# First expert layer: rows stored by token and gathered by index, in place of rows scattered to their expert

## The reference

```
gates = softmax(xf @ Wg.T)                 # xf: 2048 tokens x 256, layer-normed
topw, topi = top_k(gates, 2)
C = 538                                    # capacity of an expert
e_ord = topi.T.reshape(-1)                 # all first choices, then all second choices
cnt = position of each entry among those of its expert, in that order
buf[e, pos] = xf[token]        where cnt < C
y = gelu(buf @ W1 + b1) @ W2 + b2          # per expert: 538 rows, 256 -> 1024 -> 256
out[token] = sum over its 2 choices of topw * y[e, pos] * (cnt < C)
```

## Time and profile before

| what | us |
|---|---|
| median of 3 runs (lowest, highest) | 1897.67 (1895.84, 1907.63) |
| profiled execution, device time | 1896.24 |
| its span, first to last instruction | 1894.4 |
| PE busy in it | 1618.7 |
| DVE busy in it | 1081.3 |
| ACT busy in it | 905.7 |
| POOL busy in it | 795.1 |

### The profile page before, as it was taken

The page is one execution under the profiler, slowest core; times in us unless marked ns, Lnnn a source line. Parts: engine busy times, 40 slices in busy tenths (PEclk is TensorE's granted clock), DMA queues, the critical chain, the costliest instruction groups (busy, mean ns, idle before and its releaser), DMA issues.

```text
span 1894.4 us, 26189 instructions
## 1 busy us (share of the span) xinstructions
PE 1618.7 (85%) x9225; PEld 1114.1 (59%) x9225; DVE 1081.3 (57%) x2202; ACT 905.7 (48%) x1474; POOL 795.1 (42%) x740
## 2 busy tenths in 40 slices
PE   5954999968976999856996987999999999997997
PEld 3444999946744333346993665555555655563774
DVE  5762556567966355532545797565656666644335
ACT  2422445413346998723443664555454455431463
POOL 3053211223542554421005564576665666744106
PEclk9776999979998999968998987999999999998999
DMA  9613233030000000062113000000000000022454
GB/s 363 232 67 100 80 136 134 24 119 1 1 22 1 1 7 7 14 286 78 46 46 106 1 1 34 1 0 1 1 0 1 1 1 1 0 79 74 127 162 133
DMA packets 61879, 117.76 MB, mean 62 GB/s; under 512 B 7247, under 2 KB 50499, under 8 KB 59064
## 3 DMA queue, kind: packets, MB, share of 16 engines
q1 hardware_dynamic: 53688, 95.90, 14.5%
q0 software_dynamic: 8064, 20.19, 3.3%
HBM read 72.26 MB, written 44.89 MB: 62 GB/s over the span
## 4 chain that ended last, share of the span: by engine, by line
PE 65%; DVE 16%; POOL 6%; issue 5%; ACT 4%; DMA 4%; SPq 0%; POOLq 0%; DVEq 0%; ACTq 0%
PE psum L166 60%; DMA arena<-xb 2%; DVE arena L2399 2%; POOL arena L870 2%; DVE rounded L2328 2%; DVE arena L171 1%; DVE arena L1734 1%; POOL xb L1057 1%; POOL arena L1852 1%; PE psum L206 1%; DVE arena L2475 1%; DVE arena L187 1%; PE psum L682 1%; DVE arena L1964 1%; ACT arena L1616 1%
## 5 line engine op out<-in xcount | busy, mean ns | idle before, releaser
L166 PE MATMUL psum<-arena 128*128 (+14 forms) x5084 | 1015.3, 433 | 115.6 <-DVE arena L1725 20.5
L166 PEld LDWEIGHTS psum<-arena 128*128 128x128 f32 (+3 forms) x5084 | 586.1, 174 | 439.3 <-issue 288.1
L166 PE MATMUL psum<-rounded 128*128 128x256 f32 (+7 forms) x3072 | 531.0, 338 | 6.0 <-ACT rounded L1573 1.4
L166 PEld LDWEIGHTS psum<-rounded 128*128 128x128 f32 (+3 forms) x3072 | 407.4, 186 | 137.5 <-issue 53.3
L2503 POOL TENSOR_TENSOR arena<-arena 128x1024 f32<-128x1024 f32 (+1 forms) x111 | 262.9, 2369 | 128.7 <-ACT arena L2453 124.3
L2399 DVE TENSOR_REDUCE arena<-psum 128x1 f32<-128x512 f32 x256 | 163.5, 681 | 95.6 <-PE psum L166 94.2
L2453 ACT ACTIVATE arena<-psum 128x1024 f32<-128x1024 f32 x144 | 147.3, 1024 | 141.8 <-PE psum L166 141.1
L1616 ACT ACTIVATE arena<-psum,arena 128x1024 f32<-128x1024 f32 x128 | 134.5, 1116 | 21.8 <-PE psum L166 20.5
L870 POOL DMA_INDIRECT arena<-yb,arena x48 | 46.0, 958 | 211.9 <-DMA yb<-arena 198.4
L1210 POOL DMA_INDIRECT yt<-arena x40 | 39.8, 996 | 183.5 <-DVE arena L1173 178.0
L918 DVE SCALAR_TENSOR_TENSOR rounded<-arena,rounded 128x540 fp32r<-128x540 f32 (+1 forms) x96 | 81.8, 885 | 33.5 <-ACT rounded L1119 32.4
(11 more groups left out here) (269 smaller groups left out, 1894.0 us busy)
## 6 DMA issues: line engine op xcount, KB each, us to landing
arena<-in_w SPq DMA_DIRECT2D x8, 2048.0 KB, 8.7
arena<-xb SPq DMA_DIRECT2D x70, 128.0 KB, 2.2
yb<-arena SPq DMA_DIRECT2D x70, 128.0 KB, 1.7
arena<-in_w1u SPq DMA_DIRECT2D x4, 2048.0 KB, 15.4
xb<-arena SPq DMA_DIRECT2D x3, 2048.0 KB, 16.0
xb<-arena SPq DMA_DIRECT2D x2, 2064.0 KB, 31.7
arena<-xb SPq DMA_DIRECT2D x8, 516.0 KB
yt<-arena SPq DMA_DIRECT2D x2, 2048.0 KB, 15.2
```

The costliest lines, as they stand in the source:

```text
L166: return e.matmul(o, l, r, start=start, stop=stop, skip_group_check=True)
```

## The change

- `xb0` is now 4096 rows of 256 in the order of pairs (row 256t + 2p + k, the same row for both choices k) and 128 rows of zeros behind. SP writes it with two DMAs for each tile as soon as the tile is normed (32 DMAs of 128 KB). Only the 128 rows of zeros are blanked ahead.
- In place of slot numbers, DVE makes for each pair its block (expert times 5 + rank div 128, of 40) and its place in the block (`dve_columns0`), and a matrix of marks, 128 tokens x 128 places (`dve_marks0`). PE multiplies marks with columns that hold 16 - t and 2p + k in the block's column (`pe_marks0`, 32 products of 128 x 80, all summed in one bank), and DVE reads off the table of pair numbers by slot, 128 x 40 (`dve_ids0`). Slots without a pair get 4096, the first row of zeros.
- POOL gathers each expert's rows by that table, five indirect DMAs of 128 rows (`pool_rows0`), those of experts 0 to 2 ahead of the first result scatter, those of x + 2 ahead of expert x's result scatters. SP's `load_rows` is gone, and so are the 32 scatters.
- The same table serves the scatters of results.

The diff, without the changes of counts in later layers and the views that only name memory:

```diff
...
@@ -109,7 +109,7 @@
-        xb0, yt0 = dram("xb0", RXA, RW), dram("yt0", 2 * 128 * NT)
+        xb0, yt0 = dram("xb0", 2 * 128 * NT + 128), dram("yt0", 2 * 128 * NT)
         xb1, yb1 = dram("xb1", NB1 * 128), dram("yb1", NB1 * 128)
...
@@ -235,11 +235,11 @@
         z_tile = oR + 7680
-        N_ZERO = 16 * (3 + 2 + 3 + 2)
+        N_ZERO = 16 * (1 + 2 + 3 + 2)
...
             e.wait_ge(s_zsrc, 1)
-            for buf, rows, n in ((xb0, RXA, RW), (yt0, 2 * 128 * NT, 256), (xb1, NB1 * 128, 256), (xb3, NB3 * 128, 256)):
+            for buf, rows, n in ((xb0[2 * 128 * NT:], 128, 256), (yt0, 2 * 128 * NT, 256), (xb1, NB1 * 128, 256), (xb3, NB3 * 128, 256)):
                 bv = buf.rearrange("(a p) n -> p a n", p=128)
@@ -266,8 +266,8 @@
             settle(e, dve, e.tensor_reduce(NBD, cst("tri"), AX.X, ALU.add))
-            settle(e, dve, e.tensor_scalar(NBD, NBD, 2.0, GONE + 2.0, ALU.mult, ALU.add))
-            e.tensor_scalar(IDS, bc(cst("iota")[:, 0:NT], 2, 2), 256.0, NBD, ALU.mult, ALU.subtract)
+            for k in range(2):
+                e.tensor_scalar(PLACE[:, k:k + 1], NBD, -2.0, k - 2.0, ALU.mult, ALU.add)
             e.wait_ge(s_gate, 1)
@@ -657,10 +657,6 @@
                 pool_rstd(e, 16 + t + 1, t)
-            e.wait_ge(s_slot, 1)
-            e.wait_ge(s_zero, N_ZERO)
-            pool_scatter0(e, 0, 8)
...
@@ -894,8 +889,14 @@
         BACK_TILES = {0: 1, 1: 1, 2: 2, 4: 2, 6: 2, 8: 4, 12: 4}
-        BACK0 = dict(zip(BACK_TILES, [(s, 16) for s in s_rout] + [(s, 144) for s in s_rin[:2]] + [(s, 16) for s in s_rin[2:]]))
-        s_xg = sem("rows_blank")
+        BACK0 = dict(zip(BACK_TILES, [(s, 16) for s in s_rout] + [(s, 272) for s in s_rin[:2]] + [(s, 16) for s in s_rin[2:]]))
+        s_ip = sem("ids_product")
+        f0_m = o + 8192
+        f0_MK, f0_CL = (view(f0_m + a, n).bitcast(BF16).rearrange("p (c r) -> p c r", c=32) for a, n in ((0, 2048), (2048, 1280)))
+        f0_HIT, f0_RAMP = view(f0_m + 3328, 320).bitcast(BF16).rearrange("p (c r) -> p c r", c=16), view(f0_m + 3648, 64).bitcast(BF16)
+        f0_J40, f0_A4, f0_LIM = view(f0_m + 3712, 40), view(f0_m + 3760, 16, 4), view(f0_m + 3752, 4)
+        f0_A, f0_R = view(f0_m + 3824, 32), view(f0_m + 3856, 16).bitcast(BF16)
+        f0_AT = view(f0_m + 3880, 40)
         s_w1a, s_w1d, s_w2a, s_w2d = sem("w1_hi"), sem("w1_lo"), sem("w2_hi"), sem("w2_lo")
@@ -951,7 +952,7 @@
             xg = f0_Xg[:, x % 2]
-            e.wait_ge(s_rin[x % 2], 32 * (x // 2 + 1))
+            e.wait_ge(s_sct[x % 2], 80 * (x // 2 + 1))
             for k in range(2):
@@ -1042,38 +1043,60 @@
             settle(e, dve, e.tensor_reduce(f0_POS[:, cs], f0_T[i].rearrange("p e t -> p t e"), AX.X, ALU.add))
-            e.tensor_scalar(f0_BIG[:, cs], f0_POS[:, cs], float(CAP), 1e6, ALU.is_ge, ALU.mult)
-            settle(e, dve, e.scalar_tensor_tensor(out=f0_TO[:, cs], in0=f0_MI[:, cs], scalar=-float(CAP), in1=f0_POS[:, cs],
-                                                  op0=ALU.mult, op1=ALU.add))
-            settle(e, dve, e.scalar_tensor_tensor(out=f0_TO[:, cs], in0=f0_BIG[:, cs], scalar=8.0 * CAP, in1=f0_TO[:, cs],
-                                                  op0=ALU.add, op1=ALU.add))
-            e.tensor_copy(f0_IS[:, cs], f0_TO[:, cs]).then_inc(s_slot, 1)
-        def pool_scatter0(e, a, b):
-            for c in range(a, b):
-                e.indirect_dma_start(
-                    xb0, bass.IndirectOffsetOnAxis(f0_IS[:, c:c + 1], 0), XN[:, c % NT, :], None,
-                    bounds_check=8 * CAP - 1, oob_is_err=False).then_inc(s_sct[c // NT], 16)
-        def pool_second_ids0(e, half):
-            v = IDS[:, 8 * half:8 * half + 8, :]
-            e.wait_ge(s_sct[0], 16 * 8 * (half + 1))
-            settle(e, pool, e.tensor_scalar(v, v, 1.0, None, ALU.add))
-        def pool_ids0(e, x):
-            e.wait_ge(s_rin[x % 2], 32 * (x // 2 + 1))
-            if x == 0:
-                e.wait_ge(s_xg, 1)
-            settle(e, pool, e.tensor_scalar(f0_ID[:, x, :], f0_Xg[:, x % 2, :, 256], float(GONE), None, ALU.add))
-            e.sem_inc(s_ids, 1)
+        def dve_ramps0(e):
+            io = cst("iota")
+            for a, n in ((0, 48), (48, 48), (96, 32)):
+                e.tensor_scalar(f0_RAMP[:, a:a + n], io[:, 0:n], float(a), None, ALU.add)
+            e.tensor_scalar(f0_J40, io[:, 0:40], -40.0, None, ALU.add)
+            settle(e, dve, e.tensor_scalar(f0_LIM, io[:, 1:5], 128.0, None, ALU.mult))
+        def dve_columns0(e, i):
+            cs, k = PART_COLS[i], i // 2
+            n = cs.stop - cs.start
+            pos, blk, j, hit, cl = f0_POS[:, cs], f0_A[:, cs], f0_TO[:, cs], f0_HIT[:, 0:n, :], f0_CL[:, cs, :]
+            e.tensor_scalar(f0_BIG[:, cs], pos, float(CAP), 1e6, ALU.is_ge, ALU.mult)
+            settle(e, dve, e.tensor_tensor(f0_A4[:, 0:n, :], bc(pos, 2, 4), bc(f0_LIM, 1, n), ALU.is_ge))
+            settle(e, dve, e.tensor_reduce(blk, f0_A4[:, 0:n, :], AX.X, ALU.add))
+            e.scalar_tensor_tensor(out=f0_R[:, cs], in0=blk, scalar=-128.0, in1=pos, op0=ALU.mult, op1=ALU.add)
+            settle(e, dve, e.scalar_tensor_tensor(out=j, in0=f0_MI[:, cs], scalar=-5.0, in1=blk, op0=ALU.mult, op1=ALU.add))
+            settle(e, dve, e.tensor_tensor(j, j, f0_BIG[:, cs], ALU.add))
+            settle(e, dve, e.tensor_tensor(hit, bc(f0_J40, 1, n), bc(j, 2, 40), ALU.is_equal))
+            e.tensor_tensor(cl[:, :, 0:40], bc(cst("desc")[:, PART_TILES[i]], 2, 40), hit, ALU.mult)
+            settle(e, dve, e.tensor_scalar(cl[:, :, 40:80], hit, PLACE[:, k:k + 1], None, ALU.mult))
+        def dve_marks0(e, i):
+            cs = PART_COLS[i]
+            e.tensor_tensor(f0_MK[:, cs, :], bc(f0_RAMP, 1, cs.stop - cs.start), bc(f0_R[:, cs], 2, 128),
+                            ALU.is_equal).then_inc(s_slot, 1)
+        def pe_marks0(e, i):
+            e.wait_ge(s_slot, i + 1)
+            for c in range(PART_COLS[i].start, PART_COLS[i].stop):
+                m = mm(e, psum[:, 5, 0:80], f0_MK[:, c, :], f0_CL[:, c, :], c == 0, c == 31)
+            if i == 2:
+                m.then_inc(s_ip, 1)
+        def dve_ids0(e):
+            e.wait_ge(s_ip, 1)
+            settle(e, dve, e.tensor_scalar(f0_AT, psum[:, 5, 0:40], -256.0, 256.0 * NT, ALU.mult, ALU.add))
+            e.tensor_tensor(f0_ID.rearrange("p x a -> p (x a)"), psum[:, 5, 40:80], f0_AT, ALU.add).then_inc(s_ids, 1)
+        def pool_rows0(e, x):
+            if x >= 2:
+                e.wait_ge(s_tu, 3 * (x - 1))
+            for a in range(5):
+                e.indirect_dma_start(f0_Xg[:, x % 2, a, :], None, xb0,
+                                     bass.IndirectOffsetOnAxis(f0_ID[:, x, a:a + 1], 0)).then_inc(s_sct[x % 2], 16)
...
             pe_ranks0(e, 2)
+            for i in range(3):
+                pe_marks0(e, i)
             pe_rows(e, 0)
@@ -1124,13 +1147,21 @@
         def dve_ffn0(e):
+            dve_ramps0(e)
+            dve_columns0(e, 0)
             dve_best0(e, 1)
             e.sem_inc(s_gx, 1)
+            dve_marks0(e, 0)
             dve_place0(e, 1)
             dve_best0(e, 2)
-            dve_place0(e, 2)
             GT = f0_IDF[:, 1, :].rearrange("p (k t) -> p k t", k=2)
             e.tensor_tensor(GT, f0_M, bc(f0_M[:, 0, :], 1, 2), ALU.subtract).then_inc(s_gx, 1)
+            dve_columns0(e, 1)
+            dve_marks0(e, 1)
+            dve_place0(e, 2)
+            dve_columns0(e, 2)
+            dve_marks0(e, 2)
+            dve_ids0(e)
             e.tensor_scalar(f0_WI, f0_POS, float(CAP), None, ALU.is_lt)
@@ -1139,7 +1170,6 @@
                                                   in1=f0_WI.rearrange("p (k t) -> p k t", k=2), op0=ALU.mult, op1=ALU.mult))
-            e.memset(f0_Xg[:, :, 4, :], 0.0).then_inc(s_xg, 1)
             e.wait_ge(s_zero, N_ZERO)
@@ -1194,25 +1224,22 @@
         def pool_ffn0(e):
-            e.wait_ge(s_slot, 2)
-            pool_second_ids0(e, 0)
-            pool_scatter0(e, 8, 16)
-            e.wait_ge(s_slot, 3)
-            pool_scatter0(e, 16, 24)
-            pool_second_ids0(e, 1)
-            pool_scatter0(e, 24, 32)
-            pool_ids0(e, 0)
-            pool_ids0(e, 1)
+            e.wait_ge(s_zero, N_ZERO)
+            e.wait_ge(s_rin[0], 16 * NT)
+            e.wait_ge(s_rin[1], 16 * NT)
+            e.wait_ge(s_ids, 1)
+            pool_rows0(e, 0)
+            pool_rows0(e, 1)
             ny = 0
             for x in range(8):
+                if x < 6:
+                    pool_rows0(e, x + 2)
                 for a in range(5):
...
                     ny += 1
-                if x < 6:
-                    pool_ids0(e, x + 2)
             pool_heads(e, 1)
@@ -1225,31 +1252,23 @@
-            def load_rows(x):
-                if x >= 2:
-                    e.wait_ge(s_tu, 3 * (x - 1))
-                    e.wait_ge(s_ids, x - 1)
-                e.dma_start(f0_Xg[:, x % 2, 0:4, :], xb0[CAP * x:CAP * x + 512, :].rearrange(
```

(23 more changed lines are left out.)

## The result

| | us |
|---|---|
| before, median of 16 runs | 1897.99 (1895.36 to 1907.63) |
| after, median of 16 runs | 1883.23 (1878.27 to 1894.17) |
| ratio, 95% interval | 0.992 (0.9906 to 0.9935) |
| profiled execution after: device time, span | 1892.82, 1891.0 |

The change takes 14.8 us off the median, 0.8%, within 1% as forecast.

A forecast was written before the change was run, and what follows sets the result against it. POOL's issue of 24 scatters, then a landing and a load, bounds expert 0's start; PE bounds what follows. Rows at 153.0 instead of 168.12 save 15.1 us from 1896.24, giving 1881.1 us; range 1874 to 1887.

The forecast's parts named there:

- The bound: Between routing and expert 0: POOL's issue of 24 scatters, then landing and load, sets the start; 38 us removed.
- DVE's chain: From placing part 0 to the table of pair numbers: columns 3.1 us, marks 2.3, PE products 2.4; table at 138.8.
- The upper end of the table: Latest time for the table of pair numbers, with dearest columns and products: 141.3 us, 2.5 later than forecast.
- The part ahead: Up to the last norm before routing: as before, but 0.56 us shorter by four dropped instructions.
- The term that decides: Expert 0's fifth gather meets expert 2's weight load: rows land 8.3 us behind the load's issue, at 153.0.
- The repeated row of zeros: Expert gathers: 102 of 640 rows read the same row of zeros; no price given, left in the range.
- The escape of the fifth gather: Rival at expert 0's gathers: the fifth avoids the weight load's delay; 20.1 to 21.2 us gained, 1875 to 1876; chance 0.22.
- The second rival: At expert 0's gathers: four each wait for one split, 4.6 us in all; 11.8 us gained, 1884.4; chance 0.13.
- POOL never became the bound: Rival in the expert stage: ten indirect DMAs an expert at 3.2 us make POOL the bound, 1905.6; chance 0.05.
- The stores of tokens were no wait: Rival before expert 0: token stores land late or gathers are several times slower, so no gain, 1896; chance 0.05.

The follow-up runs named there:

- the repeated one: The changed kernel run once more, unaltered; median 1885.99 us, ratio 0.9905 to the kernel before.
- the first attempt at later splits: Changed kernel with DVE's splits of expert 0's weights waiting for POOL's semaphore count after its five gathers, passed too early; median 1882.66 us, ratio 0.9893.
- four landed gathers: Changed kernel with DVE's splits of expert 0's weights waiting until four of its gathers have landed; median 1877.61 us, ratio 0.9875.
- the combined one: Changed kernel with splits waiting for four landed gathers, padding on 128 different zero rows, and marks made eight tiles at a time; median 1874.23 us, ratio 0.987.

## Why the prediction held, point by point

**The bound.** POOL's issue of scatters set the start of the experts, and what followed moved with it: the turn is 11.0 us earlier in the first pair of profiles and 12.1 in the second, the last result scatter 11.1 and 12.3.

**DVE's chain.** Columns 3.11 (3.1 foretold), marks 2.29 (2.3), PE's 16 products 1.25 (2.4, and below my lower end of 1.6). From the end of the last norm to the table it took 21.4 us, foretold 22.2. Two differences of opposite sign are in this. The choice of part 1 began 3.84 us behind the end of the last norm, foretold 3.1, because PE's eight products ahead of it took 1.88 us (granted clock 0.64 from 117 to 123 us). In the two profiles of the kernel before they took 1.08 and 1.87 (0.70 and 0.50). PE's products on the marks made up for that. The upper end of the table adds up to 141.0 from the terms that I gave (0.5 for the columns, 1.7 for the products), not 141.3; nothing hangs on it.

**The part ahead.** I let it run as before, 0.56 us shorter. The last norm started at 117.05 to 118.3 in all eight profiles of the changed kernel and its variants, and at 116.74 and 116.90 in the two of the kernel before: 0.2 to 1.6 us later. This is a step that failed: with the 0.56 it is 2.1 us in the profiled execution. It goes with the granted clock, which from 60 to 90 us was 0.81 and 0.80 in the kernel before and 0.76 to 0.79 in the eight others; over the ten profiles the norm is never earlier where this clock is lower. The windows of the kernel before and of the profiled execution after:

```profile
60.00:90.00 30.00, 27.94 (x150) 9.50 (x147) 20.43 (x32) 8.05 (x14) 2.59 (x7) 0.81 0.57 203
```

```profile
60.00:90.00 30.00, 27.94 (x143) 10.26 (x145) 20.18 (x32) 9.30 (x17) 1.54 (x4) 0.76 0.09 32
```

Why the clock was lower there is open. The blanking is not the reason, and neither are the stores of tokens, the first of which is issued at 89.33.

**The term that decides.** The load of weights meets the gathers, as argued, and its first victim lands 8.3 us behind the load's issue, the value taken. But I took the fifth gather for that first victim. It was the third in the row, because two gathers were held by 1 us each (2.05 us in all, foretold 1.1) and POOL started 0.9 us behind the table (foretold 0.1). Its rows came 11.1 us behind the load's issue, where I had 8.3. From the table to the rows it is 17.0 us against 14.2: this is the other step that failed, and only in size. Of the 2.8 us some 1.8 are the repeated row: with the rows of zeros apart the fifth gather's came 9.3 us behind the load's issue, and the third's 7.7. With the load away T to the turn is 4.1 to 4.5 us less, with the splits away too 6.4 to 6.8 less, which shows both causes.

**The repeated row of zeros** I left without a price, with 102 rows of an expert's 640 where expert 0 has 383. It is 1.5 to 2 us on the landing of expert 0's fifth gather: 4.3 us without the load, 2.8 when the rows are apart, 8.8 against 7.0 behind the load.

**The rivals.** The escape of the fifth gather didn't happen. The second rival had four gathers beside the splits, each held by one split. POOL started later, so only two began beside them, and both were held, by 1.05 and 1.00 us, in the profiled execution and within 0.01 us again in the repeated one. Elsewhere not all were: of the two gathers that began beside the splits in the first attempt at later splits, and of the two behind four landed gathers, one was held and the other took 1.10 and 0.97. The Trainium skill's rule of the exclusive lock ("SBUF — State Buffer", section "SBUF: two separate sides") would hold every one. The rows agree with it in the pair of engines and in the length of a hold, about one split of 1.16 us (4.63 / 4), and not in how many are held. The rival's stretch from the table to the rows, 17.5 us, is nearer to the measured 17.0 than the forecast's 14.2, but by 4.6 us of holds where there were 2.05. POOL never became the bound: its ten indirect DMAs an expert left it waiting for results. The stores of tokens were no wait.

**The size.** Foretold 15.1 us less, all of it at the turn of expert 0's rows, where it was 11.0 in the profiled pair and 12.1 in the second. The 4.1 us that are missing in the first pair are the 2.1 of the part ahead and the 2.8 behind the table, less the 0.8 that the chain up to the table was shorter. Measured are 14.8 by the medians (12.3 to 17.8 by the interval). That this agrees with the forecast to 0.3 us is luck, since the stage accounts for 11 to 12. Behind the last result scatter the two profiled executions of the changed kernel were 7 to 10 us longer than the two of the kernel before, so the median execution must do better there than those two; whether the other 3 us are more than scatter stays open.

## What to carry to other kernels

When a chain is taken off one queue, write down for the moment of the new critical transfer every other transfer and every DVE instruction that the same edit moves: here the splits and the load that waits for them came to lie exactly on the gathers and cost 6.4 to 6.8 us at the turn of the rows. One wait of DVE, with which the load moves too, gives them back there, and 5.7 to 6.1 of them at the first product. Transfers that queue behind a large load pay for their place in the row, so count which of them is the last, not the first. Padding that reads one row over and over cost time of its own here; spread it, and count how much of it each transfer really has.

## What was not expected of the hardware

The part of the program behind the last result scatter, the same code in all ten profiles, took 1495.7 to 1510.9 us. The same piece of it, with 304 products in each trace, shows a part of the difference. The windows view of the kernel before, of the changed kernel and of the combined one:

```profile
721.00:771.30 50.30, 43.88 (x304) 18.17 (x297) 24.44 (x24) 37.52 (x38) 21.68 (x23) 0.97 0.03 7
```

```profile
715.90:770.40 54.50, 48.29 (x304) 19.04 (x297) 24.67 (x24) 37.60 (x38) 21.41 (x23) 0.87 0.02 6
```

```profile
701.70:751.80 50.10, 43.84 (x304) 18.10 (x297) 24.47 (x24) 37.62 (x39) 21.55 (x23) 0.97 0.03 7
```

It took 4.2 us more in the changed kernel, at a granted clock of 0.87 in place of 0.97. The clock is not all of it: the 101.2 us from 569.2 in the kernel before took 104.1 from 561.3 in the changed kernel, at 0.87 in both. An edit that moves the start of a stage by some us can so be followed by several us of either sign, and these runs don't show what decides it; the interval of 16 runs is worth more than one profile, and a stage more than a span. A count of a semaphore in POOL's queue behind indirect DMAs came while four of them were still to be worked off, 1.8 us behind the first one's start.
